# Row scales and sums of a merged graph stage moved beside the next convolution's aggregation, which starts on two tiles already on chip

## What is computed

```python
def gin_conv(x, src, dst, eps, W1, ln_g, ln_b, W2):
    agg = jax.ops.segment_sum(x[src], dst, num_segments=n)
    h = (1.0 + eps) * x + agg
    h = jax.nn.relu(layer_norm(h @ W1, ln_g, ln_b))
    return h @ W2
# graph part
h = gin_conv(x, src, dst, eps_down, W1_down, lng_down, lnb_down, W2_down)
x = layer_norm(jax.nn.relu(h + x + dir_emb[0]), ln1_g, ln1_b)
h = gin_conv(x, dst, src, eps_up, W1_up, lng_up, lnb_up, W2_up)
x = layer_norm(jax.nn.relu(h + x + dir_emb[1]), ln2_g, ln2_b)
# mixing part; t is linear attention over all nodes, 8 heads of 32
x1 = layer_norm(t + x, ln1_g, ln1_b)
h = gelu(einsum(x1, W1) + b1)
y = einsum(h, W2) + b2
return layer_norm(y + x1, ln2_g, ln2_b)
```

## Time and profile before

| | us |
|---|---|
| median of three runs (lowest, highest) | 2660.68 (2659.4, 2668.28) |
| the profiled execution | 2661.84 |
| its span, first to last instruction | 2660.1 |

### The profile page before, as it was taken

One profiled execution on the slowest core, in us unless ns is written; L12 is line 12 of the kernel. 1 busy time (PEld: TensorE's weight loads), 2 busy tenths in 40 slices (PEclk: granted clock), 3 DMA queues, 4 the chain that ended last, 5 costly groups with the idle time before them and its releaser, 6 DMA issues. The chain is left out here.

```text
span 2660.1 us, 43432 instructions
## 1 busy us (share of the span) xinstructions
PE 2101.0 (79%) x12700; PEld 1688.1 (63%) x12700; DVE 1544.3 (58%) x4190; ACT 952.5 (36%) x1814; POOL 426.6 (16%) x483
## 2 busy tenths in 40 slices
PE   7758888788943258996397799769999965999992
PEld 4446666566422247885255677548888865999992
DVE  3489999688028772221576322249999855444443
ACT  4435555356000114664152000026666530333330
POOL 0000100366001004442000000000000001333330
PEclk9989999788875558998698999889999965999996
DMA  2023333100920321221400333202222061522115
GB/s 61 17 71 117 122 125 128 37 1 1 242 63 0 105 90 52 67 65 53 97 0 6 85 94 85 66 24 59 59 59 59 12 198 57 184 72 71 47 43 155
DMA packets 90751, 196.29 MB, mean 74 GB/s; under 512 B 13993, under 2 KB 56484, under 8 KB 90670
## 3 DMA queue, kind: packets, MB, share of 16 engines
q1 hardware_dynamic: 75880, 160.70, 21.1%
q0 software_dynamic: 11520, 31.47, 3.8%
q10 hardware_dynamic: 3270, 3.20, 0.4%
HBM read 130.94 MB, written 64.39 MB: 73 GB/s over the span
## 5 line engine op out<-in xcount | busy, mean ns | idle before, releaser
L1842 PEld LDWEIGHTS experts_ps_h<-experts_xt,experts_up 128*128 128x128 f32 x2944 | 347.2, 194 | 28.8 <-issue 24.5
L1842 PE MATMUL experts_ps_h<-experts_xt,experts_up 128*128 128x128 f32 x2944 | 356.6, 278 | 5.0 <-ACT experts_xt L1876 2.9
L2491 PE MATMUL gat_ps_o<-Y,gat_prob_t 125*125 125x256 f32 x1250 | 274.3, 379 | 0.0
L1933 DVE COPY experts_up<-up 128x1024 f32 (+1 forms) x184 | 122.0, 692 | 243.7 <-ACT experts_hid L1886 156.9
L2491 PEld LDWEIGHTS gat_ps_o<-Y,gat_prob_t 125*125 125x125 f32 x1250 | 233.1, 188 | 33.8
L1141 PE MATMUL adj_ps_w<-adj_one_k,adj_one_s 128*125 128x500 bf16 x1000 | 178.0, 304 | 81.9 <-DVE adj_one_k L1072 58.6
L1854 PE MATMUL experts_ps_o<-experts_down,experts_hid 128*128 128x256 f32 x960 | 226.8, 379 | 0.3 <-issue 0.3
L2171 PE MATMUL gcn_ps_a<-Yp,gcn_adj 125*125 125x512 bf16 x625 | 205.3, 382 | 20.9 <-DMA gcn_adj<-adjacency 11.1
L1901 ACT ACTIVATE experts_down<-down 128x1024 f32 (+1 forms) x120 | 138.8, 1157 | 138.7 <-DVE experts_out L1950 76.1
L1854 PEld LDWEIGHTS experts_ps_o<-experts_down,experts_hid 128*128 128x128 f32 x960 | 173.1, 190 | 19.3 <-issue 0.5
L1141 PEld LDWEIGHTS adj_ps_w<-adj_one_k,adj_one_s 128*125 128x125 bf16 x1000 | 98.1, 137 | 131.8 <-DVE adj_one_k L1072 58.5
(11 more groups left out here) (359 smaller groups left out, 3914.6 us busy)
## 6 DMA issues: line engine op xcount, KB each, us to landing
adjacency<-adj_tile SPq DMA_DIRECT2D x25, 683.6 KB
adjacency_t<-adj_tile_t SPq DMA_DIRECT2D x25, 683.6 KB
up_adj_t<-adjacency_t SPq DMA_DIRECT2D x25, 683.6 KB
gcn_adj<-adjacency SPq DMA_DIRECT2D x25, 683.6 KB
cnt<-adjacency_t SPq DMA_DIRECT2D x25, 683.6 KB
up<-in_L_ffn_w SPq DMA_DIRECT2D x32, 512.0 KB
combine_got<-pair SPq DMA_DIRECT2D x20, 560.0 KB
down<-in_L_ffn_w SPq DMA_DIRECT2D x16, 512.0 KB
```

The lines of the kernel that those rows point to most:

```text
L1842: last = nc.tensor.matmul(ps[:, h * 128:(h + 1) * 128], w[:, k * H + h * 128:k * H + (h + 1) * 128], xt[b][:, k, :], start=(k == 0), stop= ...
L1933: last = nc.vector.tensor_copy(ups[r % 2][n][:], X.ups[n][:, bass.ds(place, 1), :].rearrange("p e w -> p (e w)"))
L2491: last = nc.tensor.matmul(ps_o[b][0:ROWS, 0:C], prob_t[:, s * ROWS:(s + 1) * ROWS], K.Y[:, s, :], start=(s == 0), stop=(s == TILES - 1))
```

## The change

Four things change in the first layer.

1. In the merged stage GpSimd keeps only the roots and `mixed_gain`. The scale rows of two normalisations (`ln1_g` of the graph part, `ln2_g` of the mixing part), the shift rows and the sum into `K.X` are made later. The normalised rows go straight to `K.X1` (which now is `K.XN`'s memory) and to a new kept tensor `K.Z2`. The direction row comes as a 65th row of the weights `wg`, against a row of ones in `hid_t`. The relu of the row sum moves from VectorE to ScalarE, ahead of `gelu`. The constant row is split into three bf16 rows, and three products over both tiles take the place of a float32 product for each tile. `att` and `res` have two buffers in place of three.
2. In the merged stage the queue loads adjacency tiles 0 and 1 of the next stage into kept buffers. `gin_up` issues tiles 2 and 3, then the eleven small loads of the second convolution (`GinUp.load`), then tile 4 and the rest.
3. `gin_up` has no products with zeros: the first product of a bank opens it and its last closes it. Its loop over tiles is written out. Copies, transposes and reductions follow one another bank by bank. VectorE does the row scales and sums there: 25 instructions over 125x1280.
4. `gin_up_tail` has no loads, no preparations and no GpSimd block; VectorE adds `K.X1` itself in L1366.

```diff
@@ MixDown.load
-        sp.dma_start(self.wg[:], D[gnn + "W2_down"]).then_inc(sem, 16)
+        sp.dma_start(self.wg[0:64], D[gnn + "W2_down"]).then_inc(sem, 16)
+        sp.dma_start(self.wg[64:65], D[gnn + "dir_emb"][0:1]).then_inc(sem, 16)
-        for n, row in enumerate((D[mix + "ln1_g"], D[mix + "ln2_g"], D[gnn + "ln1_g"], D[gnn + "dir_emb"][0])):
-            sp.dma_start(self.wide[:, n, :], row.partition_broadcast(ROWS)).then_inc(sem, 16)
+        sp.dma_start(self.wide[:], D[mix + "ln1_g"].partition_broadcast(ROWS)).then_inc(sem, 16)
@@ mix_and_down
-        att = [m.sb(f"att{i}", (ROWS, 2, C)) for i in range(3)]
+        att = [m.sb(f"att{i}", (ROWS, 2, C)) for i in range(2)]
-        res = [m.sb(f"res{i}", (ROWS, 2, C)) for i in range(3)]
+        res = [m.sb(f"res{i}", (ROWS, 2, C)) for i in range(2)]
-        hid_t = [m.sb(f"hid_t{i}", (64, WIDE)) for i in range(2)]
-        base, row, zr = ([m.sb(f"{n}{i}", (ROWS, 2, C)) for i in range(3)] for n in ("base", "row", "zr"))
+        hid_t = [m.sb(f"hid_t{i}", (65, WIDE)) for i in range(2)]
+        row = [m.sb(f"row{i}", (ROWS, 2, C)) for i in range(3)]
...
+        @block.sync
+        def _(sp):
+            for i in range(2):
+                rows_dma(sp, K.adj_in[i], K.adj_t[i:i + 1].rearrange("t p n -> (t p) n"), first_in[i])
...
@@ vector
-            v.tensor_tensor(crow[:], W.flat[:, 0, :], W.flat[:, 1, :], ALU.add).then_inc(made, 1)
+            v.memset(one_row[:], 1.0)
+            for i in range(2):
+                v.memset(hid_t[i][64:65], 1.0)
             v.memset(K.Yp[:, :, 192:256], 0.0)
+            v.tensor_tensor(crow[:], W.flat[:, 0, :], W.flat[:, 1, :], ALU.add)
+            dve.drain()
+            split3(dve, nc, crow[:], crow_rest[:], [crow_parts[:, i, 0, :] for i in range(3)])
+            dve.drain()
+            v.tensor_copy(crow_parts[:, :, 1, :], crow_parts[:, :, 0, :]).then_inc(made, 1)
...
                 v.tensor_tensor(row[s % 3][:, 0:n, :], ps_w[0:ROWS, 0:n * C].rearrange("p (u c) -> p u c", c=C),
-                                base[s % 3][:, 0:n, :], ALU.add).then_inc(row_done, 1)
+                                K.XN[:, t:t + n, :], ALU.add).then_inc(row_done, 1)
...
                 if live(s):
-                    relu(s)
+                    dve.wait_ge(relu_done, s + 1 + START)
                     moments(s, tiles(s)[1], row[s % 3], ROW)
@@ scalar
+            def relu(s):
+                n = tiles(s)[1]
+                act.wait_ge(row_done, s + 1 + START)
+                nc.scalar.activation(row[s % 3][:, 0:n, :], row[s % 3][:, 0:n, :], ACT.Relu).then_inc(relu_done, 1)
...
-                normalise(s, zr[s % 3], row[s % 3], ROW, zr_done)
+                normalise(s, K.X1[:, t:t + n, :], row[s % 3], ROW, zr_done)
...
                 if live(s - 3):
                     out(s - 3)
+                if live(s + 1):
+                    relu(s + 1)
                 if live(s - 1):
                     gelu(s - 1)
@@ gpsimd: out_gain, add_out, row_gain and direction are gone, with their calls
@@ tensor
-                for u in range(tiles(s)[1]):
+                n = tiles(s)[1]
+                for i in range(3):
+                    nc.tensor.matmul(ps_o[0:ROWS, 0:n * C], one_row[:],
+                                     crow_parts[:, i, 0:n, :].rearrange("p u c -> p (u c)"), start=(i == 0), stop=False)
+                for u in range(n):
                     bank = ps_o[0:ROWS, u * C:(u + 1) * C]
-                    nc.tensor.matmul(bank, K.ones[0:1, 0:ROWS], crow[:], start=True, stop=False)
@@ gin_up
-        adj_t = [m.sb(f"adj_t{i}", (ROWS, NODES), BF16) for i in range(4)]
+        adj_t = K.adj_in + [m.sb(f"adj_t{i}", (ROWS, NODES), BF16) for i in range(2, 4)]
...
         @block.sync
         def _(sp):
-            load_tiles(sp, adj_t, K.adj_t, arrived, used)
+            for c in range(2, 4):
+                rows_dma(sp, adj_t[c], K.adj_t[c:c + 1].rearrange("t p n -> (t p) n"), arrived[c])
+            W.load(sp, w_in)
+            load_tiles(sp, adj_t, K.adj_t, arrived, used, loaded=True)
+            sp.wait_ge(w_in, W.LOADS * 16 + START)
...
-            for i, (a, z) in enumerate(cuts):
-                zero_bank(nc, K, ps[i], z - a, start=True)
...
+                        last = nc.tensor.matmul(ps[n][:, 0:z - a], K.Yp[:, t, half * 128:half * 128 + 128],
+                                                adj_t[t % 4][:, a:z], start=(t == 0 and half == 0),
+                                                stop=(t == TILES - 1 and half == 1))
+                        if t == TILES - 1 and half == 1:
+                            last.then_inc(summed, 1)
...
-            for i, (a, z) in enumerate(cuts):
-                last = zero_bank(nc, K, ps[i], z - a, start=False)
-            last.then_inc(summed, 1)
-            pe.wait_ge(moved, len(cuts) + START)
             for t in range(TILES):
+                pe.wait_ge(moved, ((t + 1) * ROWS + 499) // 500 + START)
                 last = nc.tensor.transpose(ps[t // 4][0:ROWS, (t % 4) * 128:(t % 4) * 128 + 128],
                                            agg_t[:, t * ROWS:(t + 1) * ROWS], K.ident_f[:])
-            last.then_inc(turned, 1)
+                if t % 4 == 3 or t == TILES - 1:
+                    last.then_inc(turned, 1)
...
+            for g in range(GROUPS):
+                tiles = slice(g * GROUP, (g + 1) * GROUP)
+                v.tensor_tensor(K.X1[:, tiles, :], K.X1[:, tiles, :], each(3), ALU.mult)
+                v.tensor_tensor(K.Z2[:, tiles, :], K.Z2[:, tiles, :], each(4), ALU.mult)
+                v.tensor_tensor(K.X[:, tiles, :], K.X[:, tiles, :], each(2), ALU.add)
+                dve.drain()
+                v.tensor_tensor(K.X1[:, tiles, :], K.X1[:, tiles, :], each(0), ALU.add)
+                v.tensor_tensor(K.X[:, tiles, :], K.X[:, tiles, :], K.Z2[:, tiles, :], ALU.add)
@@ gin_up_tail: its loads, its GpSimd block and its three preparations are gone
-                dve.wait_ge(base_ready, g + 1 + START)
...
-                                    base_d[b][:, lo:hi, :], ALU.add).then_inc(o_used, 1)
+                                    K.X1[:, bass.ds(g * GROUP + lo, hi - lo), :], ALU.add).then_inc(o_used, 1)
@@ program
+            K.gu = GinUp(nc, layer, D)
             build_adjacency(nc, K, D)
-            K.X1 = sb(layer, "X1", (ROWS, TILES, C))
+            K.X1 = K.XN
+            K.adj_in = [sb(layer, f"adj_in{i}", (ROWS, NODES), BF16) for i in range(2)]
+            K.Z2 = sb(layer, "Z2", (ROWS, TILES, C))
```

More of the change, by code:

```diff
@@ L471, in mix_and_down @@
         stats, mv = m.sb("stats", (ROWS, 2, 6)), m.sb("mv", (ROWS, 2, 2))
-        half, crow = m.sb("half", (ROWS, 2)), m.sb("crow", (1, C))
+        half, crow, crow_rest = m.sb("half", (ROWS, 2)), m.sb("crow", (1, C)), m.sb("crow_rest", (1, C))
+        crow_parts, one_row = m.sb("crow_parts", (1, 3, 2, C), BF16), m.sb("one_row", (1, ROWS), BF16)
         var, neg, rstd, shift = ([m.sb(f"{n}{i}", (ROWS, 4, 2)) for i in range(4)]
@@ L564, in rows @@
                 v.tensor_tensor(row[s % 3][:, 0:n, :], ps_w[0:ROWS, 0:n * C].rearrange("p (u c) -> p u c", c=C),
-                                base[s % 3][:, 0:n, :], ALU.add).then_inc(row_done, 1)
-            def relu(s):
-                n = tiles(s)[1]
-                dve.drain()
-                v.tensor_scalar(row[s % 3][:, 0:n, :], row[s % 3][:, 0:n, :], 0.0, None, ALU.max)
+                                K.XN[:, t:t + n, :], ALU.add).then_inc(row_done, 1)
             def split(s):
@@ L712, in _ @@
             pool.wait_ge(made, 2 + START)
-            def wide(n, s):
-                return W.wide[:, n, :].unsqueeze(1).broadcast_to([ROWS, tiles(s)[1], C])
             def root(s, which):
@@ L1227, in gin_up @@
 def gin_up(nc, K):
     cuts = [(a, min(a + 500, NODES)) for a in range(0, NODES, 500)]
+    W = K.gu
     with ExitStack() as st:
         m = Memory(nc, st, "up")
-        adj_t = [m.sb(f"adj_t{i}", (ROWS, NODES), BF16) for i in range(4)]
+        adj_t = K.adj_in + [m.sb(f"adj_t{i}", (ROWS, NODES), BF16) for i in range(2, 4)]
         agg_t = m.sb("agg_t", (128, NODES))
         ps = [m.ps(f"ps{i}") for i in range(7)]
-        arrived = [m.sem(f"in{i}") for i in range(4)]
-        used, summed, moved, turned = m.sem("used"), m.sem("summed"), m.sem("moved"), m.sem("turned")
+        arrived = [m.sem(f"in{i}", start=START + (32 if i < 2 else 0)) for i in range(4)]
+        used, summed, moved, turned, w_in = (m.sem(n) for n in ("used", "summed", "moved", "turned", "w_in"))
@@ L1342, in normalise @@
                                          std_ready[n], g + 1 + START, scale, shift)
-            dve.wait_ge(w_in, loads * 16 + START)
-            v.tensor_scalar(eps1[:], eps1[:], 1.0, None, ALU.add)
-            v.tensor_tensor(direction[:], direction[:], extra[:, 0, :], ALU.add).then_inc(joined, 1)
-            v.tensor_tensor(wide[:, 1, :], wide[:, 1, :], extra[:, 1, :], ALU.add)
-            dve.drain()
```

(1 more changed line is left out.)

177 lines of the change are left out of this document (74 added, 103 removed).

## The result

The changed kernel takes 2627.9 us (median of four runs, 2626.3 to 2633.2) where the kernel before took 2664.5 beside it: a ratio of 0.987, 95% interval 0.985 to 0.989. It is faster, by 1.3% or some 35 us and not by the forecast 53; on the record's base of 2660.7 the ratio gives 2626. In the profiled executions the span went from 2660.1 to 2626.8 us, -33.3.

The account below looks back on a forecast made before the run. VectorE, closely followed by TensorE, was taken to bound the merged stage, DMA engines the aggregation. From 2660.7 us, -11.7 - 14.5 - 12.7 - 8.1 - 6.0 = -53.0 gave 2608 us; own range 2600 to 2616, with rivals A to C 2590 to 2628.

Parts of the forecast that it names:

- Merged stage: Merged stage: less GpSimd and VectorE work, but a new relu loop through ScalarE and TensorE; -6 us, ends -20 and +15.
- the term of the product in the relu loop: Merged stage, second product with its constant row: 2.9 us at 2.4 GHz, 5.4 at 1.2 GHz, about a third of steps lower.
- the other steps, where nothing is hit: Merged stage, steps without instructions stretched by GpSimd: little to lose but VectorE's relu, which the loop takes back; 0.
- +3.2: Merged stage's start: splitting the constant row before everything, six instructions of about 0.4 us, drains, three memsets; +3.2 us.
- rival B: Merged stage: the relu loop does not bind, VectorE alone sets the step; -14 us more, 2594 us; chance 0.08.
- Rival A: Merged stage: the relu loop binds harder through TensorE's lower clock; stage 15 to 20 us longer than forecast, 2625; chance 0.15.
- Tile loop: Aggregation's opening and tiles: no zeroing, tiles 0 and 1 already there; 86.7 us become 75, -11.7.
- the small loads' 6.7 us: Queue in the aggregation: issuing eleven small loads takes 6.7 us, from nine in 5.5, so tile 4 is issued near 8.3.
- rival C: Aggregation: the small loads hold up tile 4 and the opening's gain goes mostly there; +8 us, 2616; chance 0.14.
- the stretches in the tail: Tail: without GpSimd's direction row, single long runs of L1353, L113 and L1370 on VectorE go; -8.1 us.
- D: Merged stage: TensorE falls to 1.2 GHz throughout and becomes its bound; +66 us, 2674, slower than before; chance 0.03.
- E: Aggregation: scales and sums outlast the tiles, or two tiles do not land early; gains cancel within 8 us, 2661; chance 0.02.

Follow-up runs that it names:

- Experiment 5: Small loads issued at the merged stage's start, relu on ScalarE, plus four unused TensorE products while it waits for the gelu, against the changed kernel: 2610.7 us.
- Experiment 6: Kernel with small loads issued at the merged stage's start (2619.2 us), with ScalarE's relu moved behind the gelu: 2592.7 us.
- experiments 7 and 11: Constant row's parts made by GpSimd, small loads early in both: with relu on VectorE 2597.9 us (7), with relu on ScalarE behind the gelu 2593.7 us (11).
- Experiment 2: Changed kernel with the eleven small loads issued at the start of the merged stage, ahead of adjacency tiles 0 and 1: 2619.2 us.
- experiments 3: Changed kernel with relu back on VectorE and the small loads issued at the start of the merged stage: 2595.9 us.
- experiment 4: Changed kernel with the eleven small loads issued ahead of adjacency tiles 2 and 3: 2637.6 us (one run).

## Why the prediction was right or wrong

**Merged stage: wrong, -6 forecast, +2.8 measured.** The step that failed first is the term of the product in the relu loop: 2.9 us in two thirds of the steps, 5.4 in one third, taken from the mean clock of 0.79, which is 3.7 on average. In the changed kernel it was 3.97 to 5.28, on average 4.83 (the table of the seven steps), and the step 13.83 where 12.6 was forecast. The other links measured as forecast: residual to row sum 7.24 (upper end 7.2, GpSimd's L737 stretches one instruction in each of these steps), row sum 0.72, relu 0.53, gelu 0.87. I had taken the mean clock of a kernel in which TensorE ran half a step aside and put it on a chain in which TensorE pauses 3.1 to 3.9 us in each of these steps, ahead of just that product. Experiment 5 shows the size: with the pause filled the product takes 2.8 and the stage is 13 us shorter.

The second step that failed is the 0 for "the other steps, where nothing is hit". The forecast's own loop of 12.6 us was longer than the three short steps of before (10.75, 12.12 and 12.14): by its own numbers they cost 2.8 us, and they cost 6.8. The four long steps gave 0.3 us in all, where 1.1 each was forecast. Against that the start gave more: the first residual came 33.4 us after the stage's start, before it 33.8, though +3.2 stood in the sum. From the eighth residual to the end the stage is 3.3 us shorter.

Experiment 6 shows the whole: with the loop opened the stage is 152, where rival B would give 176.3 - 20 = 156. So the rest of the change was worth more than I gave it, 22 to 26 us of stage (176.3 against 154.0, 154.6, 152.0 and 149.9; how much of that is the work taken from GpSimd and VectorE and how much the shorter constant row or the clock, no run separates), and the place of one relu ate all of that. Rival A had the mechanism, named its sign in the profile and gave it 0.15; I let the row's mean speak against the row of one pause. Its own price, 15 to 20 us, was too high against the 8.8 by which the stage missed the forecast. Ahead of the loop, TensorE's first product came 4.35 us after the stage's start (491.83 - 487.48), before it 0.5; but the first residual was not later, and experiments 7 and 11 show that little of it reaches the end.

**Tile loop: wrong, -11.7 forecast, 0 measured.** The terms were issue of tile 4 at 8.3 us, and 66.3 from there. Measured: 13.3 and 73.4. The first failed by the small loads' 6.7 us, the mean of nine issues, taken for eleven that took 11.4 behind two tiles and 10.0 with none ahead. The second has two causes: tiles 4 to 7 set off together, so that tile 4 landed 7.5 us after its issue, and 246 GB/s in that execution. The 2.93 us for a tile were also somewhat too low: they count TensorE's products, and at the row's 256 GB/s a tile of 125x3125 bf16 takes 3.05, or 64 us for 21. Experiment 2 shows the term as forecast (75.5 us) once the queue is free and the pace 261. This is rival C, forecast at +8, measured at 8.7 for the whole. The rest of the 11.7 goes with the pace, of which the runs show that it moves by itself, and not what sets it.

**Rivals.** A and C came together; I had priced them as cases that exclude each other. Added up afterwards with their measured sizes, 2608 + 8.8 + 8.7, they give 2626. B is what experiments 3 and 6 reach by other means. D did not come: the clock stayed at 0.80. E did not.

**What was right.** The end of the aggregation (4.6 us, forecast 4.5), the small loads before the tail (-13.2, forecast -12.7), the stretches in the tail (-7.9, forecast -8.1; none of the three instructions above 1 us), VectorE's wide work hidden behind the tiles (36 us, ended 33 us ahead of the last product; whether it slows the loads a little is open). Of the signs that I gave, "the wait before the residual over 3 us a step" was not met by the mean of 2.4, though by the first four steps, and the stage's term was wrong; "the tile loop as long as today" was met.

**Open.** What sets the pace of the loads in an execution, and whether VectorE's wide instructions have a part in it; why the merged stage of experiment 2 is 4 us longer than the changed kernel's with the same seven steps; what makes the queue's issues slow down.

## What to carry to other kernels

A wait that is put ahead of another engine's input counts with everything behind it in that engine's list: ask first whether the two can be exchanged, as here an exchange of two neighbours gave back 26 us. A stage's mean clock is no measure for a product that stands behind a pause in every step: behind pauses of 3.1 to 3.9 us it took 4.0 to 5.3 us here, with the pause filled 2.8. So a new chain that makes TensorE wait in each step is costed near the 1.2 GHz level, and compared with every step of today, also with the short ones. And small loads belong where the queue is idle, not between two transfers that the DMA engines need to stay full (7 to 9 us here): the mean of a short burst of issues is no rate for a longer one.

## What the runs showed that I had not expected

- The queue takes 0.3 to 0.7 us for each of the first four small loads and about 1.2 us on average for the seven after them (8.2 us), with no tile ahead (experiment 4).
- With the DMA engines full, the pace of loads of 125 rows of 6250 bytes lies between 228 and 267 GB/s from execution to execution, by 15 and 18 also between two executions of one program, and a loop of 75 us moves with it by up to 8.
- Products whose result is thrown away made a stage 13 us shorter, while the granted clock rose from 0.78 to 0.92 (experiment 5).
